# Two decoder layers on one core: where the second self attention's first and last steps are done

## The chip, the core and the metric

The kernel runs on one core of a Trainium2 chip. The metric is the device time of one execution in microseconds (us), the median of several runs. TensorE (PE in the profile) multiplies matrices and writes them to PSUM; VectorE (DVE), ScalarE (ACT) and GpSimd (POOL) work elementwise; SyncE (SP) and here also GpSimd start transfers (DMAs). Each engine works its own instructions in order, and semaphores order the engines among each other.

## The reference

Two decoder layers follow each other on x of 2 x 1024 rows of 256 numbers, in float32. Each does, with a residual sum after each part: layer norm, self attention, layer norm, attention to a context of 77 rows, layer norm, a hidden layer of 4 x 256. The first layer's attention has 16 heads of 64 numbers and no mask; the second's, which matters here, has 16 heads of 16 and is causal:

```python
h = _layernorm(x, ln1_w, ln1_b)
qkv = (h @ qkv_w + qkv_b).reshape(B, T, 3, H, HD)
q, k, v = [qkv[:, :, i].transpose(0, 2, 1, 3) for i in range(3)]
attn = jnp.einsum('bhtd,bhsd->bhts', q, k) * scale
attn = jnp.where(causal[None, None], neg, attn)
attn = jnp.where(tgt_mask[:, None, None, :], neg, attn)
attn = jax.nn.softmax(attn, axis=-1)
sa = jnp.einsum('bhts,bhsd->bhtd', attn, v).transpose(0, 2, 1, 3).reshape(B, T, C)
x = x + sa @ proj_w + proj_b
```

## The kernel before, in words

The program is a row of blocks. At the end of a block every engine waits for all the others. The blocks that matter are, in this order: `hidden_layer` "ff0", `project_norm` "pf0", `thin_attention` "sa1", `project_norm` "po1", `cross_attention` "ca1".

`project_norm` multiplies a source by a weight (`product`, TensorE, L1624), adds it to x (`stats_of`, DVE, L1658), normalises (`normalise`, DVE, L1684), transposes (`turn`, TensorE, L1635) and copies out to hT (`evacuate`, ACT, L1706). Its 16 tiles of 128 rows go in nine groups: seven of two tiles, two of one. TensorE's order is product(0), product(1), turn(0), product(2), turn(1) and so on, with four banks of products. POOL adds the bias to x in four chunks of four tiles (L1607). "pf0" has 32 matmul records per two-tile group, "po1" 16.

`thin_attention` works in eight heads-and-batch groups i (NI = 8; four groups of four heads, times two batches, batch = i mod 2), each of ten units s of scores. A unit's scores (L348) are exponentiated by ACT (L412), masked on the diagonal by POOL (`affine_select`, L570), and multiplied by the values (L368). What a group needs ahead of its scores are "items" that share three PSUM banks ("front"). In the order of a list, TensorE fills a bank and DVE (with ACT's help) empties it; an item takes a bank only when the item three places before is drained:

- "p", four per group: projections of q and k (L296). ACT writes the high part to `hi` (L403), DVE the remainder to `lo` (L458).
- "v", eight in all, for both batches and all heads: the values (L304), drained by DVE to `v_buf` (L468).
- "m", twenty per group, each in two banks: raw scores of the first 33 or 59 rows (L322), of which DVE takes row maxima (L479, L481). After the last, `join` makes `m_parts`.
- "t": the transposed maxima (L331, L490).

From `hi` and `lo` SP copies rows to `q_stack` and `k_stack` (`load_stack`, 24 DMAs, L223 and L225), and after "t" the maxima (`load_max`, four DMAs, L233); POOL copies to `q_top` and `k_top` (`load_top`, eight DMAs, L526), which the "m" items read and which ACT has filled first (`clear`, L424). The list `prologue` holds what comes before the first scores: all "p" of groups 0 and 1, four "v", then the twenty "m" of group 0 with one "v" after every fifth, "t", and six "m" of group 1. All later items lie in `lanes`, beside the units.

After a group, ACT takes the output to oT (`take`, L420). Its denominators are rows of it. POOL gathers them (`take_sums`, four DMAs, L533), DVE inverts them (`invert`, L504), POOL spreads them through DRAM (`spread`, one DMA L538, a wait, four DMAs L543) and multiplies (`scale`, L550). For the last group all this stands at the block's end, after the last take.

## Time and profile before

| | us |
|---|---|
| median of 3 runs | 2044.8 (2044.79 to 2047.36) |
| the profiled execution | 2044.84 |
| its span | 2043.1 |
| TensorE busy | 1859.3 (91%) |
| VectorE, ScalarE, GpSimd busy | 1149.1, 781.6, 879.0 |

The span goes from the first to the last instruction; the execution's time is a little longer. A busy TensorE can be at half clock, so its busy share has to be read beside the granted clock: 1.00 in a stretch is 2.4 GHz throughout, 0.50 is 1.2 GHz throughout.

### The profile page before, as it was taken

The page shows a single profiled execution, that of the slowest core. Times are in us where ns is not written, and L with a number is a line of the kernel's source. Part 1 is how long each engine was busy: PE and PEld are TensorE (multiplying, and loading weights), DVE is VectorE, ACT ScalarE, POOL GpSimd, SP SyncE. Part 2 cuts the span into 40 slices and gives each one's busy share as a digit, 9 for nine tenths or more (in the row PEclk, how much of TensorE's full clock was granted, in tenths as well). Part 3 has the DMA queues.
Part 4 walks back from the last instruction along what each step waited for, and adds up shares of the span by engine and source line. Part 5 has one row for each costly group of instructions (what it writes and reads, how often), then busy time and mean ns, then how long its engine had stood idle before and what let it go on. Part 6 is the DMA issues. An engine that isn't in the chain of part 4 may idle for free. (4 is left out here: it accounts for less than half of the span.)

```text
span 2043.1 us, 27780 instructions
## 1 busy us (share of the span) xinstructions
PE 1859.3 (91%) x8972; PEld 1081.9 (53%) x8972; DVE 1149.1 (56%) x2195; ACT 781.6 (38%) x1300; POOL 879.0 (43%) x767
## 2 busy tenths in 40 slices
PE   3999999999999999979999989986798975898799
PEld 1444444444444444448555668874444433665678
DVE  4566666666666666634566443334688851687601
ACT  2344444443444444431344223221266662344340
POOL 2466666666666666660222200102146655366110
PEclk9999999999999999989999989986699997999899
DMA  1522222222323232221000010003233421000001
GB/s 52 117 62 55 62 54 61 54 64 62 70 62 69 62 70 62 63 82 35 24 1 1 1 34 24 9 22 62 42 70 76 87 46 28 8 1 1 29 16 42
DMA packets 64798, 93.99 MB, mean 46 GB/s; under 512 B 20992, under 2 KB 47132, under 8 KB 64703
## 3 DMA queue, kind: packets, MB, share of 16 engines
q1 hardware_dynamic: 60351, 86.20, 18.5%
q0 software_dynamic: 4352, 6.56, 1.5%
q8 instruction: 55, 0.90, 0.2%
q14 instruction: 40, 0.33, 0.1%
HBM read 22.84 MB, written 2.24 MB: 12 GB/s over the span
## 5 line engine op out<-in xcount | busy, mean ns | idle before, releaser
L1125 POOL TENSOR_TENSOR x<-x,sa_p_buf 128x1024 f32<-128x1024 f32 x192 | 455.2, 2371 | 165.7 <-ACT sa_p_buf L973 157.7
L973 ACT ACTIVATE sa_p_buf<-sa_score 128x512 f32<-128x512 f32 x512 | 277.7, 595 | 304.6 <-PE sa_score L900 304.3
L1036 DVE TENSOR_REDUCE sa_mx<-sa_front 128x1 f32<-128x512 f32 x512 | 319.7, 682 | 98.9 <-PE sa_front L874 98.9
L900 PE MATMUL sa_score<-sa_q_stage,sa_k_stage 128*128 128x512 f32 x1024 | 323.9, 438 | 0.4 <-DMA sa_q_stage<-x 0.4
L914 PE MATMUL sa_out<-sa_p_buf,sa_v_buf 128*64 128x512 f32 x1024 | 275.7, 617 | 0.0
L900 PEld LDWEIGHTS sa_score<-sa_q_stage,sa_k_stage 128*128 128x128 f32 x1024 | 177.7, 189 | 103.1 <-issue 71.6
L412 ACT ACTIVATE sa_p_buf<-sa_score 128x1024 f32<-128x1024 f32 (+1 forms) x160 | 141.0, 937 | 113.4 <-PE sa_score L348 113.3
L1607 POOL TENSOR_TENSOR x<-x,bias_out 128x1024 f32<-128x1024 f32 x24 | 55.6, 2348 | 269.1 <-SPq L1582 162.1
L479 DVE TENSOR_REDUCE sa_mx<-sa_front 128x1 f32<-128x512 f32 (+1 forms) x256 | 156.0, 651 | 24.9 <-PE sa_front L322 21.6
L1125 POOL TENSOR_TENSOR x<-sa_p_buf 128x1024 f32<-128x1024 f32 x32 | 77.9, 2433 | 153.8 <-ACT sa_p_buf L973 153.8
L1501 POOL TENSOR_TENSOR ca_probs<-ca_s_sb,ca_inv 128x616 f32<-128x616 f32 x64 | 77.9, 1217 | 127.4 <-DVE ca_inv L1435 127.4
L1065 DVE RECIPROCAL x<-x 128x128 f32<-128x128 f32 x128 | 111.5, 912 | 20.3 <-ACT x L986 20.3
L322 PE MATMUL sa_front<-sa_k_top,sa_q_top 59*128 59x128 f32 (+4 forms) x576 | 86.2, 366 | 37.2 <-DVE sa_mx L479 27.1
L874 PE MATMUL sa_front<-sa_k_hi,sa_q_hi 64*128 64x512 f32 x512 | 111.6, 453 | 7.0 <-DVE x L1027 2.2
L1624 PE MATMUL po_prod<-w_out,o 128*128 128x256 f32 x384 | 90.1, 393 | 29.1 <-PEq L210 20.1
L570 POOL TENSOR_SCALAR_AFFINE_SELECT sa_p_buf<-sa_p_buf 128x128 f32<-128x128 f32 x256 | 65.1, 292 | 116.3 <-ACT sa_p_buf L412 116.3
L874 PEld LDWEIGHTS sa_front<-sa_k_hi,sa_q_hi 64*128 64x128 f32 x512 | 44.7, 184 | 124.0 <-issue 62.0
L322 PEld LDWEIGHTS sa_front<-sa_k_top,sa_q_top 33*128 33x128 f32 (+1 forms) x576 | 53.0, 205 | 100.3 <-DVE sa_mx L479 78.6
L914 PEld LDWEIGHTS sa_out<-sa_p_buf,sa_v_buf 128*64 128x64 f32 x1024 | 50.8, 134 | 94.2 <-issue 93.2
L1624 PEld LDWEIGHTS po_prod<-w_out,o 128*128 128x128 f32 x384 | 74.8, 198 | 40.8 <-issue 20.5
L1358 ACT ACTIVATE ca_turned<-ca_t_ps 128x1024 f32<-128x1024 f32 x64 | 65.5, 1023 | 78.3 <-PE ca_t_ps L1304 78.3
L1817 PE MATMUL ff_ps<-ff_h_hi,ff_w_hi 128*128 128x512 f32 x192 | 77.7, 405 | 15.3 <-DVE ff_h_lo L1873 13.3
(173 smaller groups left out, 2901.8 us busy)
## 6 DMA issues: line engine op xcount, KB each, us to landing
sa_k_stage<-sa_k_hi SPq DMA_DIRECT2D x64, 256.0 KB, 4.3
sa_q_stage<-sa_q_hi SPq DMA_DIRECT2D x64, 256.0 KB, 5.1
sa_k_stage<-sa_k_lo SPq DMA_DIRECT2D x32, 256.0 KB, 4.8
sa_q_stage<-x SPq DMA_DIRECT2D x32, 256.0 KB, 5.0
x<-in_x SPq DMA_DIRECT2D x8, 512.0 KB, 7.6
sa_q_stack<-sa_hi SPq DMA_DIRECT2D x64, 64.0 KB, 2.3
sa_k_stack<-sa_hi SPq DMA_DIRECT2D x64, 64.0 KB, 2.4
ff_w<-in_L_xattn_ff_w SPq DMA_DIRECT2D x16, 128.0 KB, 2.1
```

What stands on the lines that cost most here:

```text
L322: mm = pe.matmul(bank(i, item, u)[:, c0 + lo_k:c0 + hi_k], q_top[base:base + rows_of, b, r, at], k_top[base:base + rows_of, b, r, k0 + lo_ ...
L412: nc.scalar.activation(p_buf[:, n % NPB, 2 * r:2 * r + 2, 0:cols], score_ps[r][:, :, 0:cols], ACT.Exp, scale=SCALE).then_inc(exp_done, 1)
L479: dve.tensor_reduce(mx[:, b, j, place:place + 1], fr[u][:, 0:n], AX.X, ALU.max).then_inc(drained, 1)
L874: mm = pe.matmul(front_ps[bank(item, j)][:], q_hi[r, qt * P:(qt + 1) * P], k_hi[r, half * HALF:(half + 1) * HALF], start=True, stop=True)
L900: mm = pe.matmul(score_ps[n % NSCORE][:], k_stage[:, b, j, part, kt * P:(kt + 1) * P], q_stage[:, b, j, part, h * HALF:(h + 1) * HALF], st ...
L914: mm = pe.matmul(out_ps[64 * j:64 * j + 64, :], v_buf[:, b, kt, 64 * j:64 * j + 64], p_buf[:, s % NPB, j, :], start=(kt == 0), stop=(kt == ...
L973: nc.scalar.activation(p_buf[:, s % NPB, j, :], score_ps[n % NSCORE][:], ACT.Exp, scale=SCALE).then_inc(exp_done, 1)
L1036: dve.tensor_reduce(mx[:, b, j, qt, half:half + 1], front_ps[bank(item, j)][:], AX.X, ALU.max).then_inc(drained, 1)
L1065: dve.reciprocal(recip[:, h, at], recip[:, h, at]).then_inc(inverted, 1)
L1125: nc.gpsimd.tensor_tensor(acc[:, h], prev, cur, ALU.add).then_inc(added, 1)
L1501: nc.gpsimd.tensor_tensor(probs[:, n % 2, :, 0:TC], s_sb[:, n % NS], inv[:, n % 2, :].unsqueeze(2).to_broadcast((P, U, TC)), ALU.mult).the ...
L1624: mm = pe.matmul(prod[i % NPROD][:, t, :], src[:, k, at:at + P], wt[:, k, :], start=(k == 0), stop=(k == KN - 1))
```

## The change

Three of the attention's steps move. `thin_attention` now returns what to do beside the block in front, its own block (`run`), and what to do beside the product behind it (`finish`). `project_norm` takes these as `beside` and calls them at fixed places of each engine's order.

- Beside "pf0": the attention's weight loads on SP; the clears on ACT in slot 0; from slot 2 to slot 9 one "p" and one "v" item a slot, on TensorE after the product and transpose of the slot, each after a wait for the tiles that it reads; the v_buf fill and both `load_top` on POOL after the last bias add. For this the block gives three of its PSUM banks to the front and keeps three for products instead of four.
- In the attention's own block: first the stack's loads, then the constant rows, on SP; twenty "m" items with no "v" between them, "t", six "m". The next product's weights are loaded after `load_max(0)` and no more in front of it.
- Beside "po1": for the last group `take_sums` after the first bias add, `invert` after the first group's normalising, `spread` after the second add, `scale` after the third; TensorE waits for it before the fifth group (the second batch). `scale` of the group before stays at the end of the attention's block.

```diff
+class Beside:
+    def __init__(self, banks=(), n_banks=0, sync=nothing, source=nothing, tensor=nothing, scalar=nothing, vector=nothing,
+                 gpsimd=nothing):
...
-def thin_attention(nc, name, hT, ident, key_low, causal_rows, w, oT, w_out, prefetch):
+def thin_attention(nc, name, ctx, hT, ident, key_low, causal_rows, w):
...
-    prologue = [(b, ("p", n)) for b in range(B) for n in range(NPROJ)] + [(0, ("v", n)) for n in range(4)]
-    for n, m in enumerate(maxima):
-        prologue.append((0, m))
-        if n % 5 == 4:
-            prologue.append((0, ("v", 4 + n // 5)))
-    prologue += [(0, ("t",))] + [(1, m) for m in maxima[:EARLY]]
+    SLOTS = TT // GROUP + 2
+    early = [[] for _ in range(SLOTS)]
+    for n in range(TT // GROUP):
+        b, part = divmod(n, NPROJ)
+        early[n + 2] += [(b, ("p", part)), (0, ("v", n))]
+    late = [(0, m) for m in maxima] + [(0, ("t",))] + [(1, m) for m in maxima[:EARLY]]
...
+    def run(oT, w_out, prefetch):
...
+                        load_stack(0)
+                        for base in (0, SLOT):
...
+                        load_max(0)
+                        sp.wait_ge(emptied, 1)
+                        fetch_early(sp, prefetch)
+                        for i in range(NI):
+                            if i + 1 < NI:
+                                load_stack(i + 1)
+                                load_max(i + 1)
...
+                    for i, item in late:
+                        made(pe, i, item)
...
+                    pool.memset(w_out[:], 0.0).then_inc(emptied, 1)
+                    pool.memset(recip[:], 1.0)
...
-                take_sums(NI - 1)
-                scale(NI - 2)
-                spread(NI - 1)
-                scale(NI - 1)
+                    scale(pool, oT, NI - 2)
+
+    def tensor_early(pe, slot, ready):
+        for i, item in early[slot]:
+            if item[0] in ("p", "v"):
+                ready(SLOTS - 2 if slot == SLOTS - 1 else slot - 2)
+            made(pe, i, item)
+
+    def scalar_early(act, slot):
+        if slot == 0:
+            act.wait_ge(rows_in, DMA * 2)
+            act.wait_ge(qk_in, DMA * 6)
+            for b in range(B):
+                clear(act, b)
+        for i, item in early[slot]:
+            high(act, i, item)
...
+    def gpsimd_early(pool, step):
+        if step == TT // XCHUNK - 1:
+            pool.memset(v_buf[:], 1.0).then_inc(zeroed, 1)
+            pool.wait_ge(cleared, 1)
+            load_top(pool, 0)
+            pool.wait_ge(cleared, B)
+            load_top(pool, 1)
+
+    def finish(oT):
+        def source(pe, first):
+            if first * P >= (NI - 1) % B * T:
+                pe.wait_ge(scaled, NI)
+
+        def vector(dve, slot):
+            if slot == 0:
+                invert(dve, NI - 1)
+
+        def gpsimd(pool, step):
+            if step == 0:
+                take_sums(pool, oT, NI - 1)
+            elif step == 1:
+                spread(pool, NI - 1)
+            elif step == 2:
+                scale(pool, oT, NI - 1)
...
 def project_norm(nc, shared, name, src, wts, loads, early, x, ln, hT, ident, out, prefetch=(), x_in=None, x_src=None,
-                 w_in=None, w_loads=()):
+                 w_in=None, w_loads=(), beside=Beside()):
...
-    NPROD = 4
+    NPROD = 3 if beside.n_banks else 4
...
+                        beside.gpsimd(pool, c)
...
                 for i in range(NG):
                     if KN:
+                        beside.source(pe, groups[i][0])
                         product(i)
                     if ln and i >= 1:
                         turn(i - 1)
+                    beside.tensor(pe, i, ready)
                 if ln:
                     turn(NG - 1)
+                    beside.tensor(pe, NG, ready)
...
+                    beside.vector(dve, i)
...
+                        beside.scalar(act, i)
                     evacuate(NG - 1)
+                    beside.scalar(act, NG)
...
-                project_norm(nc, norm_sems, "pf0", oT, wts, loads, True, x, True, hT, ident, None)
+                early, run, finish = thin_attention(nc, "sa1", thin_ctx, hT, ident, key_low, a["causal_rows"],
+                                                    {"qkv": by_rows(L1["qkv_w"]), "bias": column(L1["qkv_b"]),
+                                                     "bias_row": row(L1["qkv_b"])})
+                project_norm(nc, norm_sems, "pf0", oT, wts, loads, True, x, True, hT, ident, None, beside=early)
...
+            run(oT, w_out, loads)
...
+                project_norm(nc, norm_sems, "po1", oT, wts, loads, True, x, True, hT, ident, None, fetch_kv,
+                             beside=finish(oT))
```

## Rows read from the trace of the kernel before

**Rows 1.** The page, part 1: busy us, share of span, instructions.

```profile
PE 1859.3 (91%) x8972; PEld 1081.9 (53%) x8972; DVE 1149.1 (56%) x2195; ACT 781.6 (38%) x1300; POOL 879.0 (43%) x767
```

**Rows 2.** Windows: stretch, us; busy PE, PEld, DVE, ACT, POOL; clock, DMA, GB/s.

```profile
1370.00:1375.00 5.00, 0.00 (x0) 0.00 (x0) 0.00 (x0) 0.00 (x0) 0.00 (x0) 0.50 0.51 107
...
1400.00:1405.00 5.00, 4.83 (x16) 3.45 (x16) 1.97 (x5) 0.00 (x0) 0.14 (x1) 0.50 0.59 104
...
1430.00:1435.00 5.00, 4.16 (x14) 3.19 (x15) 3.00 (x5) 0.00 (x0) 0.00 (x0) 0.50 0.00 0
...
1465.00:1470.00 5.00, 5.00 (x33) 2.75 (x31) 1.98 (x6) 1.52 (x3) 1.03 (x4) 0.50 0.24 42
```

**Rows 3.** Order of time, block in front: start, us, engine line, output<-input, count, idle before.

```profile
1307.54 14.05 PE L1624 MATMUL pf_prod<-w_out,o 128*128 128x256 f32 x64 [1.11 <-PEq L1780]
...
1362.48 3.62 PE L1624 MATMUL pf_prod<-w_out,o 128*128 128x256 f32 x16
...
1368.44 0.54 PE L1635 MATMUL pf_turned<-ident,pf_normed 128*128 128x128 f32 x2 [2.12 <-DVE pf_normed L1684]
...
1369.02 0.81 ACT L1706 ACTIVATE hT<-pf_turned,ln 128x128 f32<-128x128 f32 x2 [0.58 <-PE pf_turned L1635]
...
1370.42 2.04 SPq L239 DMA_DIRECT2D sa_wqk<-in_L_xattn_qkv_w  x4
```

**Rows 4.** Order of time, front of the second self attention, its first part.

```profile
1376.79 1.91 ACT L424 ACTIVATE sa_q_top<-sa_recip 128x2048 fp32r<-128x2048 f32 x1 [6.96 <-DMA sa_recip<-in_causal_rows]
...
1388.85 0.47 ACT L403 ACTIVATE sa_hi<-sa_front,sa_bqk 128x256 fp32r<-128x256 f32 x1 [1.01 <-PE sa_front L296]
...
1389.35 0.48 DVE L458 SCALAR_TENSOR_TENSOR sa_lo<-sa_front,sa_bqk,sa_hi 128x256 fp32r<-128x256 f32 x1 [0.95 <-ACT sa_hi L403]
...
1390.39 0.48 POOL L526 DMA_DIRECT2D sa_k_top<-sa_hi  x1 [1.98 <-DVE sa_lo L458]
...
1403.80 1.11 PE L322 MATMUL sa_front<-sa_k_top,sa_q_top 33*128 33x128 f32 x8
```

**Rows 5.** Order of time, same front, maxima with values between them.

```profile
1411.13 1.29 DVE L479 TENSOR_REDUCE sa_mx<-sa_front 128x1 f32<-128x512 f32 x2 [0.35 <-PE sa_front L322]
...
1415.60 1.29 DVE L479 TENSOR_REDUCE sa_mx<-sa_front 128x1 f32<-128x512 f32 x2
...
1447.17 0.66 PE L322 MATMUL sa_front<-sa_k_top,sa_q_top 33*128 33x128 f32 x8 [0.66 <-DVE sa_v_buf L468]
...
1454.89 1.08 PE L348 MATMUL sa_score<-sa_q_stack,sa_k_stack 50*128 50x512 f32 x4
```

**Rows 6.** Groups by line, 1403.5 to 1443.9: busy us, mean ns, then idle before.

```profile
L479 DVE TENSOR_REDUCE sa_mx<-sa_front 128x1 f32<-128x512 f32 (+1 forms) x32 | 19.6, 653 | 4.9 <-PE sa_front L322 4.7
...
L481 DVE TENSOR_REDUCE sa_mx<-sa_front 128x2 f32<-128x512 f32 (+1 forms) x8 | 4.1, 555 | 1.4 <-PE sa_front L322 1.4
```

**Rows 7.** Instructions of the tile sa_q_stack: ns min/median/max of each issue.

```profile
L223 SPq DMA_DIRECT2D sa_q_stack<-sa_hi x64: 550/590/918, 1387.9 to 1657.7; - x64
```

**Rows 8.** Order of time, end of the attention and start of its product.

```profile
1694.07 2.98 POOL L570 TENSOR_SCALAR_AFFINE_SELECT sa_p_buf<-sa_p_buf 128x128 f32<-128x128 f32 x12 [0.68 <-ACT sa_p_buf L412]
...
1697.89 0.60 ACT L420 ACTIVATE o<-sa_out 128x512 f32<-128x512 f32 x1 [1.84 <-PE sa_out L368]
...
1707.17 1.93 POOL L543 DMA_DIRECT2D sa_recip<-sa_den_out  x4 [1.44 <-DMA sa_den_out<-sa_den]
...
1711.19 2.33 POOL L550 TENSOR_TENSOR o<-o,sa_recip 128x1024 f32<-128x1024 f32 x1 [2.08 <-DMA sa_recip<-sa_den_out]
...
1717.88 9.26 POOL L1607 TENSOR_TENSOR x<-x,bias_out 128x1024 f32<-128x1024 f32 x4 [4.36 <-POOLq L210]
...
1717.90 9.97 PE L1624 MATMUL po_prod<-w_out,o 128*128 128x256 f32 x32 [20.07 <-PEq L210]
```

**Rows 9.** Order of time, later in that product.

```profile
1727.64 0.73 DVE L1684 TENSOR_SCALAR po_normed<-x,po_mean_var,po_inverse 128x256 f32<-128x256 f32 x2
...
1736.71 3.62 PE L1624 MATMUL po_prod<-w_out,o 128*128 128x256 f32 x16
```

More of the change, by code:

```diff
@@ L129, in places @@
     def places():
-        order = list(prologue)
+        order = [e for slot in early for e in slot] + late
         for i in range(NI):
@@ new lines, in right, with sem @@
+    def right(n, shape, dt=F32):
+        return ctx.enter_context(nc.sbuf_tensor(f"{name}_{n}", shape, dt, side="right"))
+    def sem(n):
+        return ctx.enter_context(nc.semaphore(f"{name}_{n}"))
+    q_top, k_top = [right(n, [P, B, PAIRS, T], F32R) for n in ("q_top", "k_top")]
+    hi, lo = [right(n, [P, B, T], F32R) for n in ("hi", "lo")]
+    v_buf = right("v_buf", [P, B, KT, VALL])
+    wqk, wv = right("wqk", [P, KD, NG, 2, G * dh]), right("wv", [P, KD, D])
+    bqk, bv = right("bqk", [P, NG]), right("bv", [P, D])
@@ new lines, in thin_attention @@
+    cleared = sem("cleared")
+    zeroed, emptied = sem("zeroed"), sem("emptied")
+    front_full = sem("front_full")
+    hi_done = sem("hi_done")
+    drained = sem("drained")
+    top_in = [sem(f"top_in{b}") for b in range(B)]
+    stack_in = [sem(f"stack_in{b}") for b in range(B)]
+    max_in = sem("max_in")
+    joined = sem("joined")
+    parted = sem("parted")
+    score_full = sem("score_full")
+    exp_done = sem("exp_done")
+    selected = sem("selected")
+    pv_done = sem("pv_done")
@@ new lines, in high @@
+    def high(act, i, item):
+        if item[0] != "p":
+            return
+        g, b = divmod(i, B)
+        if i >= 2:
+            act.wait_ge(stack_in[b], DMA * NSTACK * (i // B))
+            act.wait_ge(top_in[b], DMA * NTOP * (i // B))
+        act.wait_ge(front_full, filled(i, item))
+        at = slice(item[1] * PW, (item[1] + 1) * PW)
+        nc.scalar.activation(hi[:, b, at], front_ps[PLACE[i, item, 0] % NBANK][:, 0:PW], ACT.Identity,
+                             bias=bqk[:, g:g + 1]).then_inc(hi_done, 1)
@@ new lines, in invert, with load_top @@
+    def invert(dve, i):
+        dve.wait_ge(den_in, DMA * G * (i + 1))
+        dve.reciprocal(den[:, i % 2, :], den[:, i % 2, :]).then_inc(inverted, 1)
+    def load_top(pool, i):
+        b = i % B
+        pool.wait_ge(drained, filled(i, ("p", NPROJ - 1)))
+        for j in range(G):
+            r, base = head(j)
+            for dst, at in ((k_top, G * dh + dh * j), (q_top, dh * j)):
+                pool.dma_start(dst[base:base + dh, b, r, :].bitcast(F32),
+                             hi[at:at + dh, b, :].bitcast(F32)).then_inc(top_in[b], DMA)
@@ new lines, in weighted @@
+                            for j in range(G):
+                                at = VW * (G * g + j)
+                                mm = pe.matmul(out_ps[32 * j:32 * j + 32, q0 - h * HALF:q0 - h * HALF + n], v_buf[:, b, kt, at:at + 32],
+                                               p_buf[:, unit(i, s) % NPB, j, c0:c0 + n], start=(s in (0, LOWER)),
+                                               stop=(s in (LOWER - 1, NB - 1)), skip_group_check=True)
+                            c0 += n
+                        mm.then_inc(pv_done, 1)
@@ new lines, in _ @@
+                @block.vector
+                def _(dve):
+                    for i, item in late:
+                        drain(dve, i, item)
+                    for i in range(NI):
+                        for s in range(NB):
+                            for ahead, item in lanes[s]:
+                                if i + ahead < NI:
+                                    drain(dve, i + ahead, item)
+                            if s == 5 and i >= 1:
+                                invert(dve, i - 1)
@@ L588, in wide_attention @@
+    return Beside(front_ps, NBANK, sync=sync_early, tensor=tensor_early, scalar=scalar_early, vector=vector_early,
+                  gpsimd=gpsimd_early), run, finish
 def wide_attention(nc, name, hT, ident, ones, w, oT, spare):
@@ L1563, in project_norm @@
         turned = [ctx.enter_context(nc.psum_tensor(f"{name}_turned{i}", [P, KD, GROUP * P], F32)) for i in range(2)]
+        if beside.n_banks:
+            beside.banks[:] = [ctx.enter_context(nc.psum_tensor(f"{name}_front{i}", [P, HALF], F32))
+                               for i in range(beside.n_banks)]
         loaded = shared["loaded"]
```

713 lines of the change are left out of this document (321 added, 392 removed).

## The prediction

> **What bounds the kernel now.** I read the page's busy shares first, then its slices, then the stretches around the second self attention, then the order of time at both of its ends. TensorE is busy 91% of the span [rows 1]; a change that only moves matmuls pays where TensorE stands still or runs at half clock. Two such places touch the change. The first is the stretch from the last normalised tile (ACT copies it out until 1369.02 + 0.81 = 1369.83 [rows 3]) to the first scores at 1454.89 [rows 5], 85.1 us. TensorE does nothing from 1370 to 1375, and from 1400 to 1435 it is granted half clock (0.50 of full, the 1.2 GHz level), and again so before 1470 [rows 2]. The second is from the last output copy (1697.89 + 0.60 = 1698.49 [rows 8]) to the next product's first matmul at 1717.90 [rows 8], 19.4 us, in which only POOL, one reciprocal and small DMAs work. Between the two, the loop over 80 units is the same in both kernels.
>
> **Part 1, projections and values in the block in front.** The new items of a slot are 4 matmul records for the projections and 8 for the values, of the same shape as the product's (128x256 moving columns). 64 of these take 14.05 us at full clock [rows 3], 0.22 each, so a slot costs 12 x 0.22 = 2.63 us on TensorE. In that block TensorE is the engine that runs without a break, so I count this in full: six slots (2 to 7) lie before the last product, 15.8 us, and its end goes from 1362.48 + 3.62 = 1366.10 [rows 3] to 1381.9. The slot after it is mostly free: the last transpose now waits 2.12 us for the normalising [rows 3] and would wait for 2.63 us of matmuls, 0.5 more. The evacuation ends at 1369.83 + 15.8 + 0.5 = 1386.1. Then come the last projection's matmuls (0.9), ACT's high part and DVE's low part (0.47 and 0.48 [rows 4], and some 0.3 for the hand-overs), 1388.3.
>
> The other work is covered there. ACT's four clears of 1.9 us [rows 4] lie behind the first root; they hold the second root back by about 1 us, and its transpose stands behind a whole group's 7.0 us of products. Uncovered they would cost that 1 us. DVE gets two reads more in a slot of 9.6 us, where it had some 3 us of work. Three product banks for four cost nothing while the product, not the sum, is late; if a sum were late, TensorE would wait for it once a group. The v_buf fill on POOL is done before slot 2. SP's weight loads, 5 us of idle TensorE at the border [rows 2], go under the first products.
>
> What is late next is POOL. Its eight DMAs for the second batch's tops wait for that last low part; POOL picked up such a release 0.56 us after its end (1389.35 + 0.48 to 1390.39) and issues at 0.48 us each [rows 4]: 0.56 + 8 x 0.48 = 4.4, until 1392.7. And the block can't end before POOL has left it. That exit is the first unknown. Nearest rows: after the self attention POOL's last multiply ended at 1711.19 + 2.33 = 1713.52 and the next block began at 1717.88, 4.36 us [rows 8]; at the border into the attention, where POOL had been idle, SP started 0.59 us after ACT's end [rows 3]. Bounds 0.6 and 4.4; I take 4.4, because the first border also has POOL last, with DMAs of its own behind it. The new block starts at 1397.1, and its first maxima with it; now they begin at 1403.80 [rows 4]: 6.7 us earlier.
>
> **Part 2, maxima without values between them.** From 1403.80 to the first scores are 51.1 us. The eight groups' 40 reductions are 19.6 + 4.1 = 23.7 us of DVE, with 6.3 us idle between them [rows 6]: DVE and TensorE take turns, because three banks hold one pair and a half. Four value items stand between. Between the reductions around one, DVE stops from 1411.13 + 1.29 = 1412.42 to 1415.60 [rows 5], 3.18 us for a usual 0.35, so 2.83; three of them give 8.5. The fourth stands before the transposed maxima: the next maxima start at 1447.17 [rows 5] and could at some 1445.0, 2.2 (an estimate: the transpose itself is short). Of the 10.7 I give 0.7 back, since the values' dense matmuls raised the clock for three reductions around 1438. That leaves 41.1 us: first scores at 1438.2, **16.7 us earlier**. For the clock in this stage the bounds are the present half and full. At full clock the turn-taking (6.3 idle over some 20 items, 0.33 us each) would go, 26 x 0.33 = 8.6 us less. I take half, because TensorE will have stood idle for some 9 us before it, and after less idle than that (1370 to 1375) and again at 1400 it was at half [rows 2], and because with less work than now there is less to raise it. From the first scores to the return of full clock I keep today's length (over 10 us).
>
> The Trainium skill bears on this ("TensorE: Matmul & The Clock Gate", section "Loop structure matters more than you think"): a copy out of PSUM between bursts of matmuls does not cool the array, only long waits do. The trace disagrees here: with waits under 1.4 us, each for a DVE reduction, the granted clock stayed at 0.50 for 30 us. By the page the stage would run at full clock once warm, which is the second rival.
>
> SP is moved too. It now issues the 24 stack DMAs and 8 row DMAs only after the border: 32 of 0.59 us and the gaps between them, 20 us [rows 7], and the maxima give it 33 before it must send the transposed ones, so they are covered with 13 us to spare; 0 us. The later weights (seven DMAs) stand in front of the next group's stack, which has ten units, over 30 us. Without that cover they would cost their own 3.5 us.
>
> **Part 3, the last denominators beside the product.** POOL's selections end at 1694.07 + 2.98 = 1697.05, then comes one multiply of 2.35, 1699.4, and the exit of 4.4: the product's block starts at 1703.8 for 1717.90 [rows 8], 14.1 us earlier. The bounds are again an exit of 0.6 and of 4.4. It starts at half clock as now, since the idle is 6 us; two groups take 9.97 [rows 8]. The cost is a new wait of the fifth group for the last multiply. In the block's own time: first bias add 2.3 (9.26 for four [rows 8]); four DMAs 2.0 (4.3); second add (6.7); POOL waits for DVE's reciprocal, which stands behind the first group's normalising, 1727.64 + 0.73 - 1717.90 = 10.5 [rows 9], plus 0.35; the DMA out with its pick-up 1.2 and its landing 1.4, four DMAs 1.9 [rows 8] (15.4); third add (17.7); multiply (20.1). TensorE gets to that group at 1736.71 - 1717.90 = 18.8 [rows 9]. It waits 1.3 us. The unknown is a longer POOL chain; every us goes straight into the time. Bounds: 0 if POOL gets a little ahead, and 4 if it has to wait for landings that the adds now cover. I take 1.3. **12.8 us gained.** POOL's exit of this later block is hidden: it ends some 15 us before the block.
>
> The Trainium skill speaks against this part ("SBUF — State Buffer", section "Who interferes with whom"): DVE and GpSimd share a pair of ports, and a two-input or two-port DVE instruction can block POOL for its length. No row of before has POOL's DMAs beside DVE's normalising. By the page POOL's chain could be held up by about one 0.37 us instruction at two or three of its steps, and the time would be about 1 us more.
>
> **Sum.** 16.7 + 12.8 = 29.5; 2044.8 - 29.5 = **2015.3 us**. The profiled execution took 2044.84, the median of the three runs is 2044.8, so no correction.
>
> **Rivals.**
> 1. *POOL leaves a block cheaply* when it is not at the end of a long queue of DMAs. Both borders gain up to 3.8, the second gives 0.5 back to a longer wait: 2008. For it: one border of 0.59 us. Against: the 4.36 is where POOL is last, as it will be. 0.15.
> 2. *The maxima at full clock*: 8.6 less, 2007; with a quick return of full clock in the scores another 3 or so. For it: around 1438 DVE reduced without a gap. Against: the 0.50 of 1400 and 1430 [rows 2]. 0.10.
> 3. *The colder start lasts longer.* Without the values' matmuls, the return from half to full comes several units later (or POOL's chain is longer, or the front waits for its DMAs), 7 to 12 us: 2025. For it: half clock still held at 1465, after 10 us of dense scores [rows 2]. 0.15.
> 4. *Slower.* TensorE's clock stays at half deep into the head groups. 80 units lie between 1454.89 and 1698, 3.0 us each, and TensorE is nearly full in them, so at half clock one would take some 2.5 more; the gain is used up after 12 such units, and with 20 the time is 2015.3 + 50 = 2065. Against: in the product at 1717.90 two groups took 9.97 us where full clock takes 7.03, so half clock held for only some 6 us of dense work. 0.03.
> 5. *The work is only moved.* If TensorE's items in the front block each met a wait for a drained bank (3 us a slot), 8 slots x 3 = 24 us would go there: 2039. Against: a bank has a whole group's 7 us to come free. 0.04.
>
> **How the numbers follow.** The forecast has 0.53, and 2010 to 2021 as its own range. Range of all: 2003 (rival 1 or 2 with good luck elsewhere, not both) to 2027 (rival 3), which leaves out rivals 4 and 5 and 1 and 2 together. Faster by over 0.2% (4 us, what a measurement here tells from no change) is all but rival 4 and, from rival 5, a share of 0.02 for stalls near 3.5 us a slot, where it would be the same: 0.95, 0.02, 0.03.
>
> **What would show it.** Right: in the front block TensorE without a gap and its length up by some 16 to 20 us; SP's first stack DMA some 4 us after POOL's last one; first maxima near 1397, first scores near 1438; the granted clock 0.50 in between; first matmul of the next product some 6 us after the last of the attention, and a wait of 1 to 2 us before its fifth group. Wrong: a gap before the projections in a slot, a product group waiting for sums, a block border under 1 us where POOL is last, scores that wait for a stack, or a loop of 80 units whose length differs from today's by over 3 us.

## The result and the profile after

| | before | after |
|---|---|---|
| median of the runs | 2045.82 (4 runs) | 2029.91 (2027.02 to 2033.36, 4 runs) |
| ratio | | 0.9922, 95% interval 0.9905 to 0.9940 |
| profiled execution, its span | 2044.84, 2043.1 | 2027.02, 2025.3 |

The kernel is 15.9 us faster by the medians, 17.8 by the two profiled executions. The forecast was 29.5, and its range ended at 2027. By the page of after, part 1 (answers to [rows 1]), every engine has as many instructions as before:

```profile
PE 1851.6 (91%) x8972; PEld 1078.1 (53%) x8972; DVE 1157.2 (57%) x2195; ACT 781.4 (39%) x1300; POOL 879.0 (43%) x767
```

DVE alone is busier, by 8.1 us (1157.2 for 1149.1), with as many instructions. That is the first trace of what went wrong.

The front. Order of time of after (answers to [rows 3 to 5]): first product of the block in front, POOL's last top DMA, the start of the attention's block, its first maxima, its first scores.

```profile
1310.67 14.05 PE L1686 MATMUL pf_prod<-w_out,o 128*128 128x256 f32 x64 [1.11 <-PEq L1853]
...
1395.55 0.48 POOL L375 DMA_DIRECT2D sa_q_top<-sa_hi  x1
1399.15 0.58 SPq L428 DMA_DIRECT2D sa_q_stack<-sa_hi  x1
1399.15 0.95 POOL L565 MEMSET w_out<- 128x1024 f32 x1 [3.12 <-POOLq L1642]
...
1399.45 1.12 PE L283 MATMUL sa_front<-sa_k_top,sa_q_top 33*128 33x128 f32 x8 [7.08 <-PEq L1642]
...
1441.20 1.08 PE L476 MATMUL sa_score<-sa_q_stack,sa_k_stack 50*128 50x512 f32 x4
```

From the first product to the first scores are 1441.20 - 1310.67 = 130.5 us. Before they were 1454.89 - 1307.54 = 147.35 [rows 3, 5], so the front gained 16.8. The groups of reductions between the first maxima and the transposed ones (answer to [rows 6]; busy us, mean ns, idle before; 7.47 of the 8.8 is the wait for the very first) and the windows (answer to [rows 2]) show how:

```profile
L342 DVE TENSOR_REDUCE sa_mx<-sa_front 128x1 f32<-128x512 f32 (+1 forms) x32 | 19.5, 652 | 6.1 <-PE sa_front L283 6.1
L344 DVE TENSOR_REDUCE sa_mx<-sa_front 128x2 f32<-128x512 f32 (+1 forms) x8 | 4.1, 554 | 8.8 <-PE sa_front L283 8.8
```

```profile
1400.00:1405.00 5.00, 2.74 (x18) 1.97 (x16) 3.34 (x6) 0.44 (x1) 0.99 (x2) 0.50 0.64 101
1430.00:1435.00 5.00, 2.26 (x15) 1.56 (x13) 3.24 (x8) 0.00 (x0) 0.00 (x0) 0.50 0.01 2
...
1455.00:1460.00 5.00, 4.71 (x42) 3.10 (x36) 2.53 (x5) 2.02 (x3) 0.00 (x0) 0.77 0.02 3
1460.00:1465.00 5.00, 4.78 (x32) 2.37 (x30) 4.42 (x8) 4.02 (x7) 2.16 (x5) 1.00 0.21 36
```

The reductions cost what they did, and the idle between them is 6.1 + 1.3 us for 6.3. The granted clock is 0.50 in the maxima. It comes back to full between 1455 and 1460 (0.77 in that stretch, 1.00 in the next), some 16 us after the first scores. Before it came back as late: 0.50 from 1465 to 1470 [rows 2] and 0.90 from 1470 to 1475, with the first scores at 1454.89.

The end. Order of time of after (answers to [rows 8, 9]): the last output matmuls, the last multiply and the last take of the attention's block, then the product's block up to its fifth group, and the cross attention's first matmul.

```profile
1682.54 2.77 PE L496 MATMUL sa_out<-sa_p_buf,sa_v_buf 128*32 128x384 f32 x24 [0.86 <-POOL sa_p_buf L578]
...
1683.34 2.35 POOL L399 TENSOR_TENSOR o<-o,sa_recip 128x1024 f32<-128x1024 f32 x1
...
1685.36 0.60 ACT L536 ACTIVATE o<-sa_out 128x512 f32<-128x512 f32 x1 [3.00 <-PE sa_out L496]
...
1695.10 2.34 POOL L1668 TENSOR_TENSOR x<-x,bias_out 128x1024 f32<-128x1024 f32 x1 [9.42 <-POOLq L415]
1695.12 9.39 PE L1686 MATMUL po_prod<-w_out,o 128*128 128x256 f32 x32 [9.81 <-PEq L415]
...
1710.18 2.36 POOL L1668 TENSOR_TENSOR x<-x,bias_out 128x1024 f32<-128x1024 f32 x1
1710.41 6.75 DVE L1741 TENSOR_SCALAR po_var_eps<-po_mean_var 128x2 f32<-128x2 f32 x1
1712.49 2.34 POOL L399 TENSOR_TENSOR o<-o,sa_recip 128x1024 f32<-128x1024 f32 x1
1714.79 2.33 POOL L1668 TENSOR_TENSOR x<-x,bias_out 128x1024 f32<-128x1024 f32 x1
...
1718.42 1.11 PE L1697 MATMUL po_turned<-ident,po_normed 128*128 128x128 f32 x4 [6.02 <-DVE po_normed L1752]
...
1719.32 5.72 PE L1686 MATMUL po_prod<-w_out,o 128*128 128x256 f32 x16
...
1742.47 0.76 PE L1299 MATMUL ca_t_ps<-ctxT,wk 96*128 96x154 f32 x4 [1.15 <-PEq L1642]
```

Two things stand here that no step of the forecast had. POOL ends its multiply at 1685.69 and the next block begins 9.4 us later, not 4.4. And a DVE instruction on two numbers a row takes 6.75 us; the median of the 18 of its tile is 0.168. It ends 0.04 us after the last of three POOL instructions that follow each other without a gap. TensorE waits 6.02 us for the normalised tiles behind it, and comes back at a lower clock (0.76 granted from 1715 to 1718.4, 0.50 to 1722, 0.74 to 1725, then 1.00): the transposes take 1.11 instead of 0.60, the product 5.72 instead of 3.62.

Stage by stage, in the profiled executions (minus is earlier):

| stretch | before | after | difference |
|---|---|---|---|
| start to pf0's first product | 1307.54 | 1310.67 | +3.1 |
| to the first scores | 147.35 | 130.53 | -16.8 |
| to the end of the last take | 243.60 | 244.76 | +1.2 |
| to po1's first product | 19.41 | 9.16 | -10.25 |
| to the cross attention's first matmul | 39.86 | 47.35 | +7.5 |
| to the end of the span | 285.3 | 282.8 | -2.5 |

The first and the last are stages whose code is the same. In the other profiles below with that code they vary as much: pf0 starts between 1306.4 and 1310.7, and the last stage takes 282.5 to 285.7 us.

The +1.2 of the third row belongs to the fourth. The last 24 output matmuls took 2.77 us here (granted clock 0.76 from 1680 to 1685) and 1.62 us before and in every other profile. So the last take came 1.15 us later, but POOL's last multiply, which starts when its selections end, did not. Without this the loop is as long as before (243.6 us) and the border 10.3 us, as it is in a1_repeat.

### The profile page after: what moved, and what is told of

Same layout as the page of the kernel before. It is cut to its first block and busy times, and to the rows that moved or that the text cites. A ratio compares the mean times of both kernels' runs of the same rounds, so it can differ in the third digit from the quotient of the medians.

```text
span 2025.3 us, 27798 instructions
## 1 busy us (share of the span) xinstructions
PE 1851.6 (91%) x8972; PEld 1078.1 (53%) x8972; DVE 1157.2 (57%) x2195; ACT 781.4 (39%) x1300; POOL 879.0 (43%) x767
## 5 line engine op out<-in xcount | busy, mean ns | idle before, releaser
L283 PE MATMUL sa_front<-sa_k_top,sa_q_top 59*128 59x128 f32 (+4 forms) x576 | 87.8, 372 | 46.0 <-DVE sa_mx L342 29.5
L1686 PEld LDWEIGHTS po_prod<-w_out,o 128*128 128x128 f32 x384 | 76.6, 203 | 31.7 <-issue 10.7
```

Source lines behind the costliest of these rows:

```text
L283: mm = pe.matmul(bank(i, item, u)[:, c0 + lo_k:c0 + hi_k], q_top[base:base + rows_of, b, r, at], k_top[base:base + rows_of, b, r, k0 + lo_ ...
L1686: mm = pe.matmul(prod[i % NPROD][:, t, :], src[:, k, at:at + P], wt[:, k, :], start=(k == 0), stop=(k == KN - 1))
```

## The experiments

Theory C: POOL pays for leaving a block by the number of DMAs it has issued in it. Theory D: a run of POOL instructions without a gap holds a DVE instruction of a certain kind until the whole run is over, and the moved multiply has joined adds to such a run. The expectations of the a and b runs call theory D "theory P"; their theory W is that TensorE really waits for POOL's chain, and theory F that the exit costs the same whatever the number of DMAs. Theories A and B of a1 only ask whether the exit is the same in every execution. Theory E (c2) is that only the instruction on two numbers a row is held. "Exit" is the time from the end of POOL's last instruction in a block to its first in the next. All ratios are to runs of the kernel before on the same chip.

**a1_repeat: the changed kernel again**, for the comparisons within this set. No edit.

> The changed kernel again, nothing altered, for a second profile and as the partner of the others of this set. If the profiled 2027.0 was a fortunate execution, this one lies at 2028 to 2032. Two places are in question. Exit: from the attention's last copy (ACT) to the next product's first matmul the first profile has 9.2 us where I had forecast 5.3; theory A says POOL's exit from that block always takes some 9 us after its last multiply, theory B that it varies from execution to execution (then this profile shows another value by 2 us or more). Product block: theory P (a DVE tensor_scalar can't start while POOL's elementwise instructions follow each other) expects the one long DVE instruction of 6 to 7 us again, and 47 us for the block.

Measured: 2027.8, ratio 0.9912 (0.9898 to 0.9926). Exit 9.41 again, DVE's long instruction 6.17, product's block 46.6 us. Both are properties of the kernel, not of one execution.

One thing is not. The attention's loop took 246.9 us here. In after the granted clock was 0.50 for the first 16 us of scores; here it was 0.50 for 24 us (0.80 from the 24th to the 28th) in the same kernel. The loop was as long, 246.9 to 247.2 us, in the other three profiles with 24 us at half clock (a2_old_tail, b3_bias_first, c1_best), and 243.2 to 245.6 in those with less, b1_more_dmas aside. Why the full clock comes back at two different places is open. Some 3 us of any comparison of single executions below are this.

**a2_old_tail: parts 1 and 2 alone.**

```diff
+                    take_sums(pool, oT, NI - 1)
                     scale(pool, oT, NI - 2)
+                    spread(pool, NI - 1)
+                    scale(pool, oT, NI - 1)
...
+                    invert(dve, NI - 1)
...
-                             beside=finish(oT))
```

> Undoes part 3 alone: the last group's gather, reciprocal, spread and multiply go back to the end of the attention's block. Parts 1 and 2 stay. The first profile says that the front brought 16.8 us and part 3 only 2.8 net (10.2 at the border, less 7.5 in the product's block). If both are right, this is 2 to 4 us slower than the changed kernel and 12 to 15 faster than the kernel before. Rival: part 3 is worth what it was forecast to be (12.8) and the front less, then it is 10 or more slower than the changed kernel. Exit after POOL's last multiply: 4.4 us again if the exit depends on what POOL did last.

Measured: 2035.2, ratio 0.9948 (0.9934 to 0.9962). The expectation of 2 to 4 us slower was missed, because it took the exit of the old tail to be 4.4 us. Order of time, last multiply and next block:

```profile
1698.38 2.33 POOL L399 TENSOR_TENSOR o<-o,sa_recip 128x1024 f32<-128x1024 f32 x1 [2.06 <-DMA sa_recip<-sa_den_out]
1710.86 9.25 POOL L1672 TENSOR_TENSOR x<-x,bias_out 128x1024 f32<-128x1024 f32 x4 [10.15 <-POOLq L415]
```

So the long exit does not come from the moved tail. It comes with parts 1 and 2, which took sixteen POOL DMAs out of this block (136 before, 120 here). Before, the tail had a stop of 2.07 us among its first four DMAs, after the 128th of the block, and then an exit of 4.36 [rows 8]:

```profile
1698.78 0.52 POOL L533 DMA_DIRECT2D sa_den<-o  x1 [1.73 <-ACT o L420]
1701.37 1.49 POOL L533 DMA_DIRECT2D sa_den<-o  x3 [2.07 <-issue]
```

Here there is no stop, and an exit of 10.15. The product's block takes 39.8 us. Beside this front part 3 is worth 2035.2 - 2027.8 = 7.4 us by the medians, and 6.1 by the two stages that it touches: 12.8 at the border (23.11 for 10.30) less 6.75 in the product's block (39.84 for 46.59).

**a3_early_bias: the bias adds of the product done in the attention's block**, so that nothing adjoins the multiply. The next product's weights are loaded before the transposed maxima for this.

```diff
+                    add_bias(pool)
                     for i in range(NI):
...
-                        nc.gpsimd.tensor_tensor(x[:, tiles, :], x[:, tiles, :],
+                        if not biased:
+                            nc.gpsimd.tensor_tensor(x[:, tiles, :], x[:, tiles, :],
```

> The product block's four bias adds on POOL (9.3 us) are done in the attention's block instead, during the maxima, where DVE only reduces from PSUM; the next product's weights are loaded before the transposed maxima for that. In the product's block POOL then has only the gather, the spread and one multiply. Theory P (POOL's run of adds and the multiply holds DVE off): DVE's long instruction shrinks from 6.8 to at most the one multiply, 2.4 us, the product's block from 47 to 40 or 41, and the time falls by 6 to 7 us. Theory W (TensorE really waits for the multiply, the end of POOL's chain of gather, spread and landings): the chain is shorter by one add only, 2.3 us, so the gain is 2 us at most. If the adds slow the maxima, the front's 41 us from first maxima to first scores grow, which either theory allows but neither expects.

Measured: 2020.1, ratio 0.9873 (0.9858 to 0.9887). Product's block 1737.33 - 1697.27 = 40.1 us, and no DVE instruction of the small kind over 0.42 us: the 7.5 us are gone with the run. The exit stayed at 9.4. But the front grew from 41.8 to 43.9 us, for the same reason at a new place. The adds run 9.24 us from 1422.65, the join of the maxima falls into them, and its DVE instruction ends as they do:

```profile
1422.65 9.24 POOL L2117 TENSOR_TENSOR x<-x,bias_out 128x1024 f32<-128x1024 f32 x4 [23.69 <-DMA ln<-in_L_xattn_ln_b]
```

```profile
1429.62 2.31 DVE L358 TENSOR_TENSOR sa_mx<-sa_mx 128x16 f32<-128x16 f32 x1
```

The reductions out of PSUM in these 9 us were not held.

**a4_gap: the same work in the same order, with gaps in POOL's run.** POOL waits for the third normalised group before the multiply, and for the fourth before the last add.

```diff
+                        if c == 2 and beside.gap:
+                            pool.wait_ge(normed.sem, normed.since(3))
                         beside.gpsimd(pool, c)
+                        if c == 2 and beside.gap:
+                            pool.wait_ge(normed.sem, normed.since(4))
```

> Nothing moves; POOL only waits before its last multiply until the third group is normalised, and before its fourth add until the fourth is. Theory P: DVE's instruction lasts no longer than the add that it meets (2 to 2.4 us), the multiply ends some 2 us later, and the fifth group waits for it; the block is 42 to 44 us for 47 and the time 3 to 5 us less, although POOL has been made later. Theory W: everything that makes POOL later makes the block longer, so the time is up by 1 to 3 us.

Measured: 2023.6, ratio 0.9877 (0.9859 to 0.9895); product's block 42.3 us for 46.6. DVE's small instruction now ends with the one POOL instruction that it meets, twice:

```profile
1709.67 2.36 POOL L1671 TENSOR_TENSOR x<-x,bias_out 128x1024 f32<-128x1024 f32 x1
1710.18 1.88 DVE L1748 TENSOR_SCALAR po_var_eps<-po_mean_var 128x2 f32<-128x2 f32 x1
...
1713.35 2.34 POOL L400 TENSOR_TENSOR o<-o,sa_recip 128x1024 f32<-128x1024 f32 x1 [1.32 <-DVE po_normed L1759]
1714.97 0.74 DVE L1748 TENSOR_SCALAR po_var_eps<-po_mean_var 128x2 f32<-128x2 f32 x1
```

1710.18 + 1.88 is 1712.06, and the add ends at 1712.03; 1714.97 + 0.74 is 1715.71, and the multiply ends at 1715.69. Adding two waits to POOL made the kernel faster, by 4.2 us against a1_repeat. The fifth group still waits 1.76 us for the later multiply.

**b2_tops_on_sp: 48 of POOL's top DMAs given to SP** (63 left in the block, for 111).

```diff
+                                if i + 2 < NI:
+                                    load_top(sp, i + 2)
...
-                            if s == LOWER + 1 and i + 2 < NI:
-                                load_top(pool, i + 2)
```

> The changed kernel with the 48 DMAs to the tops of groups 2 to 7 issued by SP instead of POOL; POOL has 63 left in the attention's block. Theory C: the exit costs by the number, about 0.4 + 0.08 per DMA from the two values known, so 5.5 us instead of 9.4, and the time is some 4 us less, if SP brings the tops in time. Theory F: the exit stays at 9 us or more. If SP's queue, now 25% longer, is late, the units wait for tops or stacks and the loop grows; either theory allows that, and the loop's length (244.8 us from first scores to last copy) shows it.

Measured: 2025.5, ratio 0.9905 (0.9891 to 0.9919). The exit is 5.50 us, the number expected:

```profile
1689.00 2.34 POOL L1675 TENSOR_TENSOR x<-x,bias_out 128x1024 f32<-128x1024 f32 x1 [5.50 <-POOLq L422]
```

The long DVE instruction stays (6.30), and the block's 46.8 us with it: the two costs are independent. The 4 us show at the border (6.39 for 10.30) and not clearly in the time: the ratio's interval overlaps those of the changed kernel (0.9922 and 0.9912).

**b1_more_dmas: 24 small POOL DMAs more in the block** (135), in six groups of four with a wait after each.

```diff
+                                    for n in range(4):
+                                        pool.dma_start(spare_out[4 * (i - 1) + n], den[:, (i - 1) % 2, :]).then_inc(spare_in, DMA)
+                                    pool.wait_ge(spare_in, DMA * 4 * i)
```

> The changed kernel with 24 more DMAs on POOL's own queue inside the attention's loop (copies of the denominators to an unused buffer in DRAM, four in each of six groups; the output is unaffected). In the traces so far POOL took 9.4 us to leave the attention's block after 111 DMAs of its own there, 10.2 after 120, 3.1 to leave the block in front after 16; and in the kernel before, with 136, 4.4 at the exit but also 2.1 us of standstill just after its 128th DMA. Theory C (POOL settles its DMAs when 128 have gathered or when it leaves a block, and the exit costs by the number still open): with 135 there is a standstill of 2 us after the 128th and the exit falls to some 4 us, so the next block starts 4 to 5 us after the last copy instead of 9.2, and despite 11.6 us more of POOL work inside the loop, which is hidden, the time is 3 to 5 us less than the changed kernel's. Theory F (the exit has its price by what code follows, or by the time since the last DMA): 9 to 11 us again, time equal or longer.

Measured: 2069.9, ratio 1.0138 (1.0099 to 1.0176). The time tells nothing of theory C, and the 3 to 5 us less that I expected did not come: the loop grew to 287.4 us. POOL waited 8.5 us in all for the added DMAs, in six places before selections that the units need, and TensorE's granted clock was 0.74 to 0.87 in the 40 us stretches from 1480 to 1680, where a1_repeat has mostly 1.00. I had priced neither. The places do tell: a stop of 1.20 us right after the 128th DMA of the block, and an exit of 4.60, near the 4.36 of before:

```profile
1709.81 1.03 POOL L384 DMA_DIRECT2D sa_den<-o  x2
1712.03 0.98 POOL L384 DMA_DIRECT2D sa_den<-o  x2 [1.20 <-issue]
...
1724.85 2.34 POOL L401 TENSOR_TENSOR o<-o,sa_recip 128x1024 f32<-128x1024 f32 x1
1731.79 2.34 POOL L1674 TENSOR_TENSOR x<-x,bias_out 128x1024 f32<-128x1024 f32 x1 [4.60 <-POOLq L417]
```

**b3_bias_first: a3 with the next product's weights loaded before the stacks**, so that the adds end before the join.

```diff
+                        sp.wait_ge(emptied, 1)
+                        fetch_early(sp, prefetch)
                         load_stack(0)
...
-                        sp.wait_ge(emptied, 1)
-                        fetch_early(sp, prefetch)
```

> The kernel with the bias adds in the attention's block, now with the next product's weights loaded before the stacks, so that the adds run in the first 12 us of the maxima. In the last run with these adds the time from first maxima to first scores was 43.9 us instead of 41.8, since the adds still ran when DVE had to join the maxima (tensor_tensor and tensor_scalar instructions of 16 columns). Theory P (only such DVE instructions are held off by POOL, reductions from PSUM are not): 41.8 again, and the time is 2 us less. If the reductions are held too, the front stays at 43 to 44 or grows.

Measured: 2021.3, ratio 0.9887 (0.9869 to 0.9905). The front is back at 1436.93 - 1395.17 = 41.8 us, as it should be if POOL's adds held the join (they start at 1401.50 and end at 1410.75). The 2.1 us don't show in the time: the ratio's interval overlaps that of a3 (0.9873), and the profiled loop was 246.9 us, one of those with 24 us at half clock, for 245.6 in a3.

**b4_part3_alone: the old front, the new tail** (127 POOL DMAs in the block).

```diff
+    late = [(b, ("p", n)) for b in range(B) for n in range(NPROJ)] + [(0, ("v", n)) for n in range(4)]
+    for n, m in enumerate(maxima):
+        late.append((0, m))
+        if n % 5 == 4:
+            late.append((0, ("v", 4 + n // 5)))
...
-                project_norm(nc, norm_sems, "pf0", oT, wts, loads, True, x, True, hT, ident, None, beside=early)
+                project_norm(nc, norm_sems, "pf0", oT, wts, loads, True, x, True, hT, ident, None)
```

> Part 3 alone: projections, values and maxima stand in the attention's block in their old order, the last group's denominators go beside the next product. If the parts add up, it is 11 to 15 us slower than the changed kernel (the front's 16.8 us less noise) and 2 to 8 us faster than the kernel before. Theory C: POOL has 127 DMAs in the attention's block, one short of the 128, so no standstill and a long exit, 10 to 11 us, and part 3 gains even less than the 2.8 us seen, about 1 us. Theory F: exit 4.4 as before, and part 3 brings 14.1 - 7.5 = 6.6 us.

Measured: 2042.9, ratio 0.9987 (0.9978 to 0.9996). The exit is what theory C gave. The border is 7.8 us shorter than before (11.61 for 19.41), and with the long DVE instruction (6.22) the product's block is 6.5 longer (46.38 for 39.86), so little is left:

```profile
1709.78 2.34 POOL L1690 TENSOR_TENSOR x<-x,bias_out 128x1024 f32<-128x1024 f32 x1 [10.73 <-POOLq L421]
```

**c2_eps_on_act: the changed kernel without the instruction that was held.** EPS goes into ScalarE's square root.

```diff
-                    dve.tensor_scalar(ve[:, u, 0:size], mv[:, u, 0:size, 1], EPS, None, ALU.add).then_inc(var_done.sem, 1)
+                    ins.then_inc(var_done.sem, 1)
...
-                    nc.scalar.activation(sd[:, i % 2, 0:size], ve[:, i % 2, 0:size], ACT.Sqrt).then_inc(sd_done.sem, 1)
+                    nc.scalar.activation(sd[:, i % 2, 0:size], mv[:, i % 2, 0:size, 1], ACT.Sqrt, bias=eps[:]).then_inc(sd_done.sem, 1)
```

> The changed kernel without the small DVE operation po_var_eps (EPS goes into ScalarE's square root as a bias). Theory D (POOL's run of add, multiply, add holds whatever tensor_scalar of DVE meets it): the hold moves to the next one, the normalising (256 numbers a row, tile po_normed), one of which takes 4 to 7 us; the product's block stays at 46 to 47.5 us to the cross attention's first matmul, and the time is 2026 to 2030. Theory E (only the 2-number operation is hit): no DVE instruction over 1.5 us in that block, its length 40 to 42, time 2021 to 2023.

Measured: 2021.7, ratio 0.9884 (0.9868 to 0.9900). The hold moved to the next instruction of the kind, as theory D has it:

```profile
1707.67 6.47 DVE L1750 TENSOR_SCALAR po_normed<-x,po_mean_var,po_inverse 128x256 f32<-128x256 f32 x2
```

```profile
1706.72 2.37 POOL L1668 TENSOR_TENSOR x<-x,bias_out 128x1024 f32<-128x1024 f32 x1
1709.03 2.34 POOL L399 TENSOR_TENSOR o<-o,sa_recip 128x1024 f32<-128x1024 f32 x1
1711.33 2.34 POOL L1668 TENSOR_TENSOR x<-x,bias_out 128x1024 f32<-128x1024 f32 x1
```

The record covers two instructions of 0.37 us. The run ends at 1713.67 and the record at 1714.14, so the first was held to the end of the run and the second followed it. The product's block took 45.4 us, so theory E (only the small instruction is hit) falls, though the time is where E had it. The time expected by theory D was 4 us too high. The small operation had also stood in DVE's chain of every group in every block: the first self attention starts at 36.8 instead of 37.8, the stretch from pf0's first product to the first maxima takes 88.0 instead of 88.8, and the product's block is 1.2 shorter than in a1_repeat (2.0 than in after). The loop of 243.6 us, 3.2 shorter than a1_repeat's, had the earlier return of the clock (within the 12th to 16th us of scores). No run tells whether the edit has a part in that.

**c1_best: b3 and b2 together.**

> The bias adds in the attention's block, the next product's weights loaded first, and 48 of POOL's top DMAs given to SP: the three edits that each gained, in one kernel. If they add up: first scores 41.8 us after the first maxima, the last multiply to the next block 5.5 us instead of 9.9 (63 DMAs of POOL in the block), the product's block to the cross attention's first matmul 39.7 to 40.1, no DVE instruction over 1 us in it, time 2021.25 - 4.4 = 2017, range 2014 to 2020. If SP becomes late with its stacks by the 48 DMAs beside the weights (rival), a unit's scores wait and the time is at or over 2021.

Measured: 2019.9, ratio 0.9876 (0.9856 to 0.9895). From the last multiply's end (1689.25) to the product 5.5 us, the product's block 40.0 us, the first scores 41.7 after the first maxima: each as expected. The time is 2.9 above the sum, within the range. b2's 4 us show only in part beside b3's 2021.3, and the two intervals overlap; the profiled loop was 247.2 us, again with 24 us at half clock.

**c3_best_eps: c1 and EPS as in c2.**

> c1_best and EPS as ScalarE's bias together. The small operation and its hand-over leave DVE's chain of every group; that counts only where a block waits for its first or last group. Expected: 0 to 2 us faster than c1_best, some 2015 to 2017, and the product's block behind the attention 39.5 us. If the square root with a bias from memory is slower on ScalarE and late (rival): the same as c1_best or 1 us more.

Measured: 2012.1 (2009.6 to 2013.0), ratio 0.9834 (0.9819 to 0.9849): faster than expected by 3, and 17.9 us (0.9%) faster than the changed kernel's 2029.9. The best version run. The product's block took 40.9 us, not the 39.5 expected: its first two groups took 9.99 us for c1's 9.16. Against c1 the profiled execution is 7.1 us shorter, of which 0.8 lies between pf0's first product and the first scores and 4.0 in the loop, with its earlier return of the clock; another 4.2 lie before pf0, where the kernels without the edit differ by as much. So how much of it is the edit's is not shown.

```profile
1677.97 2.37 POOL L406 TENSOR_TENSOR o<-o,sa_recip 128x1024 f32<-128x1024 f32 x1
...
1685.85 9.99 PE L1695 MATMUL po_prod<-w_out,o 128*128 128x256 f32 x32 [7.05 <-PEq L422]
...
1726.70 1.37 PE L1307 MATMUL ca_t_ps<-ctxT,wk 96*128 96x154 f32 x4 [1.15 <-PEq L1650]
```

## Why the prediction was wrong

**Parts 1 and 2 were right.** "First scores at 1438.2, 16.7 us earlier": in after they came at 1441.20, since pf0 itself started 3.1 late, but counted from pf0's first product they were 16.8 earlier. That stretch took 130.5 or 130.6 us in seven other profiles with this front, 129.7 and 129.8 without the small DVE operation, and 132.6 in a3. The block in front grew as worked out: its last product ended 74.9 us after its first began, forecast 1381.9 - 1307.54 = 74.4. From the first product to the first maxima are 88.8 us, forecast 1397.1 - 1307.54 = 89.6, with the exit of 4.4 measured at 3.12. From the first maxima to the first scores are 41.75, forecast 41.1. The half clock in the maxima was taken rightly, against rival 2.

**The step "the exit of 4.4" of part 3 failed.** It read a price off one row [rows 8] as if it were fixed, and took the present 4.4 us for the upper bound. The row was right and the reading wrong: the exit depends on what POOL issued in the block, and the change itself alters that. In the runs:

| POOL DMAs in the block | 16 | 63 | 111 | 120 | 127 | 135 | 136 |
|---|---|---|---|---|---|---|---|
| exit, us | 3.1 | 5.5 | 9.4 | 10.15 | 10.7 | 4.6 | 4.36 |
| kernel | after, pf0 | b2 | after | a2 | b4 | b1 | before |

Up to 127 the exit rises, by about 0.08 us a DMA between 63 and 127. It is as much for the nine DMAs that a2 has beyond after (0.74 us; 288 KB) as for the 16 of b4 (1.3 us; 64 KB each), so the number fits better than the bytes. In the two blocks with more than 128 there is a stop (1.20 and 2.07 us) right after the 128th, and then a short exit. So before had been just past that point, and parts 1 and 2, which moved 16 DMAs to the block in front, brought it just below. What is counted or settled there I can't say; that more DMAs make the exit dear is shown by b2 against after, that the tail has no part in it by a2. The border took 10.3 us with the last matmuls at their usual length, where the forecast had 1703.8 - 1698.49 = 5.3: the 5.0 are the exit. The profile of after has 9.16 at the border and the other 1.15 in the loop.

**The step "It waits 1.3 us" of part 3 failed, and it was the larger one.** The block grew by 7.5 us, where 1.3 were forecast. POOL's chain itself came as worked out: the multiply ended 1714.83 - 1695.10 = 19.7 us into the block, forecast 20.1. The error was to look only at how DVE could hold POOL, and not at how POOL holds DVE. The working had DVE at its durations of before, while three POOL instructions stood side by side for 7 us over DVE's chain. TensorE lost 6.02 us in waiting and then 2.1 + 0.5 us to the lower clock that followed, less 1.1 us by which the block's first two groups and their wait were shorter than before. By the time it reached the fifth group, at 1719.32, the multiply had long ended, so this took the place of the 1.3. Without the hold the wait forecast is there: 1.54 us in c1, 1.83 in c3. a3 (no run: 40.1 us), a4 (gaps: 42.3) and c2 (the hold moves) show it. The trace of before had it already: of the 18 small instructions one took 1.546 us for a median of 0.170, and another 0.85:

```profile
1726.32 0.85 DVE L1673 TENSOR_SCALAR po_var_eps<-po_mean_var 128x2 f32<-128x2 f32 x1
```

It ended as POOL's four adds did (1717.88 + 9.26 = 1727.14 [rows 8]). I had read the group's mean, not its longest.

The Trainium skill ("SBUF — State Buffer", section "Who interferes with whom") says that the shared pair of ports goes to whoever issues first, and that the other is blocked fully. I had drawn only one direction from it, that DVE holds POOL. The traces agree with the other one too: tensor_scalar instructions, which the same section counts among those that can take both ports, had records of 6.75, 6.30 and 1.88 us (6.47 for two in c2), and a DVE instruction with two SBUF inputs one of 2.31 us in a3, while reductions out of PSUM ran beside the same adds. The section speaks of one instruction's length; here the hold lasted for a whole run of three. No run shows the ports themselves.

**The remainder.** 5.0 (exit) + 6.2 (DVE held, beyond the 1.3) - 0.1 (front) + 0.6 (the stages without an edit) = 11.7, which is 29.5 - 17.8 of the profiled execution. The median lies another 2.9 above that execution. A loop like a1_repeat's would be 2.1 us longer; whether the other executions had it no trace shows. Rival 3 named a time in this region, by a later return of the clock or a longer POOL chain. The chain was not longer, and in the profile of after the clock came back as before; in a1_repeat it did come back 8 us later, so something of rival 3 is in the time, though the misses above are not it. Of rivals 4 and 5 nothing is seen: the clock is back at full within 28 us of the first scores in every profile, and TensorE has no waits for banks in the block in front.

## What to carry to other kernels

When work is moved beside an engine's other work, look at the longest instance of each instruction there, not at its mean: a long one tells which neighbour can hold it, and a run of POOL instructions without a gap can hold a 0.17 us DVE instruction for the whole run. Break the run (a4), or do it where DVE only reduces out of PSUM (b3). The price of a block's border is not a constant where POOL starts DMAs: count POOL's own DMAs since the last border before and after the edit, and give DMAs to SP where it has room.

## What the runs showed of the hardware

- A POOL run of three instructions of 2.3 us held one DVE instruction through all three (6.75 us); the profile shows no gap between the three.
- Not every DVE instruction is held. Beside the four adds of before (1717.88 to 1727.14) a sum with one input from PSUM took 0.69 us at 1724.53, two statistics 0.75 and their aggregation 0.25, as without POOL beside them.
- A POOL fill that reads nothing took part in a hold: in the block in front of after, the v_buf fill took 4.15 us from 1319.87, right behind the last bias add, and pf_var_eps, the sister of po_var_eps, 4.33 us from 1319.72. It ended with the fill. TensorE waited only 0.59 us there.
- POOL's exit from a block rose from 3.1 us at 16 own DMAs to 10.7 at 127, and was 4.4 to 4.6 past 128, after a stop inside the block.
- After 6.02 us of standing still TensorE's next transposes and product took 1.11 and 5.72 us for 0.60 and 3.62 (granted clock 0.50 from 1718.4 to 1722); after the 1.15 and 1.76 us of a4 they took 0.65 and 3.72 (1.00 throughout from 1710 to 1728).
- One and the same kernel had the granted clock back at full 16 us after the first scores in one execution and 24 to 28 us after in another, and its loop was 2.1 us longer.
